# Another order of the 208 items in a steady attention step

## The reference, cut to what matters

```python
scores = jnp.einsum('bhqd,bhkd->bhqk', Q, K) / math.sqrt(hd)   # + alibi in the first
scores = jnp.where(causal[None, None], scores, -jnp.inf)
attn = jax.nn.softmax(scores, axis=-1)
out = jnp.einsum('bhqk,bhkd->bqhd', attn, V)
```

## Time and profile before

| | before |
|---|---|
| median of 3 runs | 2570.25 us (2568.62 to 2571.12) |
| the profiled execution | 2568.78 us |
| its span, first to last instruction | 2566.9 us |
| TensorE matmul busy | 2326.3 us, 91% |
| VectorE busy | 1917.9 us, 75% |
| ScalarE busy | 1516.4 us, 59% |
| GpSimd busy | 579.8 us, 23% |
| attention: first m to last exponential | 384.5 to 1985.5 us |

### The profile page before, as it was taken

One profiled execution on the slowest core, in us unless ns is written; L12 is line 12 of the kernel. 1 busy time (PEld: TensorE's weight loads), 2 busy tenths in 40 slices (PEclk: granted clock), 3 DMA queues, 4 the chain that ended last, 5 costly groups with the idle time before them and its releaser, 6 DMA issues. The chain is left out here.

```text
span 2566.9 us, 52951 instructions
## 1 busy us (share of the span) xinstructions
PE 2326.3 (91%) x18274; PEld 1266.1 (49%) x18275; DVE 1917.9 (75%) x4030; ACT 1516.4 (59%) x3290; POOL 579.8 (23%) x845
## 2 busy tenths in 40 slices
PE   3299987999999999999999999999999883999997
PEld 2155544444444444444444444444443662788886
DVE  6767758988998998999998999998993573233332
ACT  2033323677777787777787777777778461222221
POOL 4412101121111111111111111111000266423223
PEclk9599997999999999999999999999999996999999
DMA  4157766553443443322322322322020894343433
GB/s 156 62 161 207 222 193 98 86 104 76 72 77 73 78 78 67 70 56 46 66 54 52 64 53 55 63 48 61 31 78 26 284 299 186 64 77 76 78 74 70
DMA packets 168302, 246.55 MB, mean 96 GB/s; under 512 B 52392, under 2 KB 125240, under 8 KB 162244
## 3 DMA queue, kind: packets, MB, share of 16 engines
q0 software_dynamic: 38304, 112.51, 23.2%
q1 hardware_dynamic: 122404, 120.68, 15.9%
q10 hardware_dynamic: 7380, 10.48, 1.4%
HBM read 120.19 MB, written 122.36 MB: 94 GB/s over the span
## 5 line engine op out<-in xcount | busy, mean ns | idle before, releaser
L1411 DVE TENSOR_REDUCE a_mx<-banks 128x1 f32<-128x512 f32 (+3 forms) x2560 | 1378.5, 603 | 127.3 <-PE banks L1240 58.8
L1371 ACT ACTIVATE a_p<-banks 128x512 f32<-128x512 f32 (+3 forms) x2560 | 1177.6, 541 | 331.0 <-PE banks L1255 201.3
L1334 PE MATMUL banks<-a_p,a_v 128*32 128x512 f32 (+3 forms) x5120 | 597.8, 542 | 1.0 <-ACT a_p L1371 0.6
L1240 PE MATMUL banks<-a_k,a_q 48*128 48x512 f32 (+7 forms) x1600 | 340.4, 428 | 10.0 <-ACT a_p L1371 2.4
L1255 PE MATMUL banks<-a_q,a_k 50*128 50x512 f32 (+7 forms) x1600 | 332.3, 426 | 11.6 <-DVE a_mx L1411 4.4
L1240 PEld LDWEIGHTS banks<-a_k,a_q 52*128 52x128 f32 (+1 forms) x1600 | 154.6, 184 | 207.3 <-DVE a_mx L1411 164.2
L1255 PEld LDWEIGHTS banks<-a_q,a_k 54*128 54x128 f32 (+1 forms) x1600 | 152.3, 184 | 201.0 <-DVE a_mx L1411 144.9
L2103 ACT ACTIVATE e_hT<-banks 128x256 fp32r<-128x256 f32 x72 | 27.6, 383 | 308.5 <-PE banks L2029 278.9
L1240 PE MATMUL banks<-a_k,q 48*128 48x512 f32 (+7 forms) x896 | 191.5, 432 | 9.1 <-DMA a_k<-aug_rows 3.4
L2042 PE MATMUL banks<-w,e_hT 128*128 x576 | 184.1, 421 | 12.1 <-DVE e_hT L2143 12.1
L1255 PE MATMUL banks<-q,a_k 50*128 50x512 f32 (+7 forms) x896 | 186.3, 428 | 6.9 <-ACT a_p L1371 2.9
(11 more groups left out here) (263 smaller groups left out, 2505.9 us busy)
## 6 DMA issues: line engine op xcount, KB each, us to landing
expert_rows<-a_zeros POOLq DMA_DIRECT2D x132, 258.0 KB, 5.2
a_k<-ka_parts POOLq DMA_DIRECT2D x42, 256.0 KB, 6.2
e_x<-expert_rows SPq DMA_DIRECT2D x72, 129.0 KB, 2.8
expert_rows<-e_y SPq DMA_DIRECT2D x72, 128.0 KB, 2.1
qa_parts<-m_part SPq DMA_DIRECT2D x16, 512.0 KB, 4.7
ka_parts<-m_part SPq DMA_DIRECT2D x16, 512.0 KB, 5.1
va_tiles<-m_va SPq DMA_DIRECT2D x8, 1024.0 KB, 5.0
qb_parts<-m_part SPq DMA_DIRECT2D x16, 512.0 KB, 4.7
```

The lines of the kernel that those rows point to most:

```text
L1240: ins = pe.matmul(outs[j][:, 0:w], q_op[o][part, p, qt * P:(qt + 1) * P], keys_of(r, k0)[part, kp, k0:k0 + w], start=True, stop=not diagonal)
L1334: ins = pe.matmul(ps_o[VW * h:VW * h + VW, c0:QB], v_op[o][:, kt, hk * VW:hk * VW + VW], prob[:, (n * GH + h) % NPB, c0:QB], start=(kt == ...
L1371: nc.scalar.activation(prob[:, (2 * n + j) % NPB, c0:QB], ps[(slot + j) % RING][:, c0:QB], ACT.Exp, scale=SCALE).then_inc(s_ex, 1)
L1411: v.tensor_reduce(mx[:, j, p, qt, k0 // WIDE:k0 // WIDE + 1], ps[banks[j]][:, 0:w], AX.X, ALU.max).then_inc(s_md, 1)
```

## The change

The string `ORDER` is replaced by another of the same length, with the same 80 m, 80 s, 40 v, 4 r and 4 t. Nothing else differs; each letter's item, its instructions, its semaphores and the number of its buffers are as before.

```diff
 ORDER = (
-    "smvsmsssmvmsmsvmsmvmsmvsmsmsmvmsmvssmsmvsmsvsmsmsvmsmvsmmvmssvmsmvssmvmsmsvsmsmvmsmmsmvs"
-    "mmrtsmsvsmmvsmsvmmsvssmsmsmvsmmrvtsmsvmmsmvsmssmvmsmsvsmmsmsmvmsstrmsmvsmsvmsmvsmvmssvms"
-    "ssmvmsmsmvmsmvmssvmssmsmsvvmssrt"
+    "msvsmsssmvmsmsvmsmvmsmvsmsmsmvmsmvssmsmvsmsvsmsmsvmsmvsmmvsmsvmssvmsmmsvsmssmvmmsmsvsmsv"
+    "rmmssmmvsmmvmsmvtsmsvsmsmsmvsmmrvtsmsvmsmsvmsmmssvmsmvsmmssmsvmstmsvsmsmsmvmsmvsmsvssmmv"
+    "msmrvmsmsvsmmvsmsvsmsmssvmvmsstr"
 )
```

## The result

The changed kernel took 2582.84 us (median of seven runs, 2578.55 to 2586.18) against 2571.60 us of the kernel before (seven runs, 2568.62 to 2574.15): a ratio of 1.0044, with a 95% interval of 1.0034 to 1.0054. It is slower, by 11 us, where 7 us less were forecast. The profiled execution took 2582.17 us, its span 2580.3 us.

A forecast was written before the change was run, and what follows sets the result against it. TensorE and VectorE were taken to bound the steady steps by holding each other up. Terms of -0.24 and -0.27 made -0.51 us a step, -7.1 us over 14 steps: 2563 us against the median 2570.25, range 2553 to 2565.

The forecast's parts named there:

- What bounds, and where it can move: TensorE and VectorE hold each other up; only the attention steps, 1449 us, can move, 1371 of them in steps 1 to 14.
- The forecast's own sign against this: Time ahead of 537 us or behind the attention moving by over 1 us would disprove that only the steps can change.
- First term: VectorE's gaps ahead of m, places 57 to 207, priced by s items between two m: 5.40 to 5.16, -0.24 us a step.
- the six svs: s, v, s between two m, at places 73, 85, 110, 157, 187, 195: 5 x 0.44 us, the one at 73 nothing.
- The class "one s": Places from 57 on with one s between two m: 28 in the new string, 0.034 us of VectorE gap each.
- The three ssv: Three places in the new string with s, s, v between two m: 0.30 us of VectorE gap each.
- Second term: End of a step, t now ahead of r: VectorE's 0.27 us wait for the t goes, -0.27 us a step.
- Third term: Places where an r or t moves: GpSimd's split for the first r still in time, priced at nothing (0 to +0.5 us).
- Fourth term: v items stand 11.5 items behind their last exponential, before 10.3: nothing to -0.3 us a step, taken as nothing.
- the slower one: The svs places decide: at 0.66 us for all six, +1.31 us a step, 2588 us; slower band given chance 0.27.
- The gaps only move: TensorE's work comes late elsewhere, so a closed gap reopens at the next place: no change, 2570 us; no-change chance 0.26.

## Why the prediction was wrong

- **What bounds, and where it can move**: right. Only the steady steps changed with the order (11.8 of the 13.4 us of span). The forecast's own sign against this, over 1 us ahead of 537, did come (2.3 us), but by step 0's clock; behind the attention it was -0.6. In the two traces the clock stayed at its full level in the steady steps. Gaps belong to places, but only as long as the whole order stays.
- **First term, the gaps by class (-0.24 us a step)**: the step that failed. The gaps were priced at 5.16 us and came to 7.30, and places 58 to 205, measured in two parts, made +0.73 us of time (0.32 + 0.41). By my own sub-classes the six svs were priced at 2.20 us and came to 2.53. That is nearly right in sum, but by luck: single ones were none shown, 1.07, 0.34, 0.35, 0.29 and 0.48. The class "one s" was priced at 28 x 0.034 = 0.95 and came to 2.53: 0.31, 0.64 (with an r), 0.30, 0.58, 0.70. The three ssv were priced at 0.90 and came to 1.24. So the mean over a class of places in one order isn't a price in another. That most one-s places had been free because of what stood ahead of them is my reading; no run tests it.
- **The method under it** failed too: it took a gap for its price. Gaps of places 57 to 207 in step 2 rose by 1.90 us in the changed kernel for +0.76 of time, by 1.02 with 58 to 108 for +0.32, by 0.72 with 146 to 205 put back for +0.05, and by 0.69 with 146 to 198 for +0.44; with 109 to 145 they fell by 0.23 for -0.39. Moving an m forward by 0.21 to 0.24 us (m 83, m 52, m 93) was worth nothing. In the changed kernel part of the 1.90 is made up in the same step: gaps under 0.15 us fell from 1.30 to 0.80 us, and VectorE was busy 0.5 us less.
- **Second term, the exchanged turn (-0.27)**: the wait at the end of the step did go, as forecast, and brought nothing in the order of before (97.96 and 97.94 us for 97.97). I had named what came next and priced it at nothing: that price, 0.27 us, was the error.
- **Third term, r and t**: right as to GpSimd. Its split was done at 677.64 and used at 678.54, a slack of 0.90 us, and what the profile names as ending TensorE's wait there is an exponential. But an r alone ahead of an m is part of the gap of 0.64 at place 89, which I hadn't priced.
- **Fourth term, the values**: wrong sign. Standing 11.5 items behind their exponentials instead of 10.3, they waited more (2.9 us for 1.5), for a distance in items says nothing of when ScalarE gets there. What that cost is not shown.
- **The rivals**: the slower one had the sign, and 2582.84 lies in its band (2576 to 2590, chance 0.27), which the range left out; but it had not the place. The svs places as a whole were not dear. Two of the six (187 and 195) do stand where 146 to 198 loses; the largest single price is the ssv at 201. "The gaps only move" was right for every gap that was tried alone by an exchange of neighbours (the turn, m 83, m 52, m 93), and was the rule that I should have set against my own second term.

What is settled: the loss comes out when 146 to 205 are put back (98.02), 0.55 us of it can be made with three letters, and 0.44 with 146 to 198. That 58 to 78 and 79 to 108 cost 0.32 us together, and that neither helps if put back alone, is settled too: the second costs 0.8 us behind either, and the first gains its 0.30 us only ahead of the second. With 79 to 108 put back the 0.80 us go, but the 0.30 gained turn into 0.33 lost. What stays open: why 79 to 108 and 146 to 198 cost what they do, why the prices of 146 to 198 and 199 to 201 overlap, and what TensorE's longer waits for ScalarE have to do with it. Afterwards the later of two engines at the next m explains a seam; no rule came out that forecasts a new order.

The best orders found are the old one with places 109 to 145 of the new: 0.9991 (0.9982 to 1.0000), and the same with two exchanges, 0.9990 (0.9981 to 0.9999). Both are at the edge of what can be told from no change.

## What to carry to other kernels

Where two engines hold each other up through a short ring of buffers, the idle time ahead of an instruction is not what it would bring to remove it: ask when the instruction behind it could start, and if that one waits for the same engine, the gap only moves. Compare two orders by the time at which a numbered item starts, measured from the start of its loop step, in both engines; that is exact to 0.03 us here where whole runs spread over several us. Look at the granted clock before a long step is put down to the order. And don't take an average price of a pattern from one order into another: the state in which the pattern is met is most of the price.

## What the runs showed that I had not expected

- Two v items side by side are cheaper for TensorE than apart: 1.21 us for one of 512 and one of 128 columns, 1.35 with an m between. But two long ones in a row cost 0.84 us a step by starving VectorE.
- VectorE's busy time fell from 89.25 to 88.71 us with the same instructions. In step 2 the 160 reductions were 0.3 us shorter in sum (96.23 for 96.53), and overlaps were 0.2 us more (10.95 for 10.77). So busy and idle time of two orders don't compare exactly. A reduction that starts a few hundredths of a us late still overlaps the one before it, and such slips count as busy. The overlap itself is seen in the row at 666.23: two reductions in 1.29 us, where each lasts 0.68. The Trainium skill ("VectorE: DVE Perf Modes", The DRAIN you can't avoid) adds that an operation which is not held starts earlier than the end of the pipe; this trace agrees.
- A delay can heal by itself: m 110 was 1.69 us late in the run with 146 to 198, and m 122 was level again. Much of it was taken up at m 114, m 118 and m 119 (0.35, 0.37 and 0.79 us), where VectorE had stood idle in the order before (0.38, 0.30 and 0.86 us): here a gap was slack for what came late ahead of it.
- All 19 long steps of the traces lie under a granted clock of 0.50, and 16 of them begin just ahead of the same m 109. One execution was 6 us longer by them (146 to 205 put back), about half of what the whole change made.
- Three letters of 208 made +0.55 us a step, nearly three quarters of what the whole new string did.
